# A four-layer GNN kernel on one core: fifteen spare matmuls behind each item of the two GGNN passes

## What is computed

```python
h = relu(x @ node_proj_w.T + node_proj_b)
for l in range(2):
    trans = einsum('nh,tdh->tnd', h, edge_W[l])       # 8 edge types
    msgs = trans[edge_type, src]                      # one row of 128 per edge
    agg = segment_sum(msgs, dst)                      # 200000 edges into 6250 nodes
    h = relu(gru_cell(agg, h, ...))
y = h @ out_w.T + out_b
```

## Time and profile before

| | us |
|---|---|
| device time, median of 3 runs | 12535.24 (12531.92 to 12542.11) |
| span of the profiled execution, first to last instruction | 10787.3 |
| the two GGNN passes within the span, first to last product | 2806 to 6783 |
| busy in the span: PE / DVE / POOL / ACT | 6086.2 / 5239.6 / 4871.8 / 1520.2 |

### The profile page before, as it was taken

One profiled execution on the slowest core, in us unless ns is written; L12 is line 12 of the kernel. 1 busy time (PEld: TensorE's weight loads), 2 busy tenths in 40 slices (PEclk: granted clock), 3 DMA queues, 4 the chain that ended last, 5 costly groups with the idle time before them and its releaser, 6 DMA issues. The chain is left out here.

```text
span 10787.3 us, 166167 instructions
## 1 busy us (share of the span) xinstructions
PE 6086.2 (56%) x60710; PEld 5248.2 (49%) x60711; DVE 5239.6 (49%) x7210; ACT 1520.2 (14%) x4256; POOL 4871.8 (45%) x5701
## 2 busy tenths in 40 slices
PE   4666659997433334443333333586999635545554
PEld 3333339995233333323333333486999634444444
DVE  7888878885211111121122222597888743323333
ACT  3666640001100000000000000132000001101101
POOL 2111110001577777757777777001000147777775
PEclk7777779998666666666666666555999867767776
DMA  1000032223222122221111111475322112222222
GB/s 46 0 0 0 0 46 83 83 83 118 79 66 66 53 66 66 66 72 53 52 52 52 52 52 52 163 292 190 112 93 92 63 54 79 79 80 79 73 79 73
DMA packets 322858, 798.38 MB, mean 74 GB/s; under 512 B 157570, under 2 KB 196012, under 8 KB 303436
## 3 DMA queue, kind: packets, MB, share of 16 engines
q1 hardware_dynamic: 147804, 423.30, 11.6%
q0 software_dynamic: 153216, 312.49, 10.2%
q10 hardware_dynamic: 21744, 61.34, 1.4%
HBM read 714.98 MB, written 81.79 MB: 74 GB/s over the span
## 5 line engine op out<-in xcount | busy, mean ns | idle before, releaser
L984 POOL DMA_INDIRECT ggnn_edges_G<-trans_d,ggnn_edges_rid x3136 | 2975.5, 949 | 1199.3 <-issue 955.1
L1097 PE MATMUL ggnn_edges_PS<-ggnn_edges_OH,ggnn_edges_G 128*128 128x128 f32 x6272 | 1176.8, 373 | 2317.1 <-DMA ggnn_edges_G<-trans_d,ggnn_edges_rid 2207.2
L1097 PEld LDWEIGHTS ggnn_edges_PS<-ggnn_edges_OH,ggnn_edges_G 128*128 128x128 f32 x6272 | 1136.7, 285 | 2361.7 <-issue 2360.2
L984 POOL DMA_INDIRECT mpnn_edges_G<-msg_d,mpnn_edges_rid x1568 | 1499.8, 956 | 659.5 <-issue 473.0
L1053 DVE TENSOR_TENSOR acc<-acc,ggnn_edges_PS 128x128 f32 x224 | 64.6, 288 | 2510.7 <-PE ggnn_edges_PS L1097 2510.7
L1081 PE MATMUL mpnn_edges_PS<-wt_late,mpnn_edges_at 128*128 128x256 f32 x1568 | 545.3, 522 | 682.1 <-DVE mpnn_edges_G L1040 339.9
L620 ACT ACTIVATE prep_OJF<-prep_OJ,prep_fld 128x98 bf16<-128x98 bf16 x3136 | 848.9, 362 | 555.0 <-DVE prep_OJ L676 555.0
L1081 PEld LDWEIGHTS mpnn_edges_PS<-wt_late,mpnn_edges_at 128*128 128x128 f32 x1568 | 414.8, 272 | 794.1 <-DVE mpnn_edges_G L1040 361.1
L826 PE MATMUL prep_PS<-prep_OJF,prep_OHr 128*128 128x490 bf16 x1582 | 580.7, 549 | 211.5 <-DVE prep_OHr L705 211.5
L1040 DVE TENSOR_TENSOR mpnn_edges_G<-mpnn_edges_G,mpnn_edges_PS 128x1792 f32<-128x1792 f32 x112 | 226.3, 2020 | 878.9 <-DMA mpnn_edges_G<-msg_d,mpnn_edges_rid 702.0
L1018 DVE SCALAR_TENSOR_TENSOR ggnn_edges_OH<-dstI,ggnn_edges_itm,ggnn_edges_PS 128x896 f32<-128x896 f32 x448 | 491.6, 1144 | 228.7 <-issue 164.1
(11 more groups left out here) (454 smaller groups left out, 10933.6 us busy)
## 6 DMA issues: line engine op xcount, KB each, us to landing
ba_rows<-slot_d SPq DMA_DIRECT2D x49, 3136.0 KB, 11.4
HB<-slot_d SPq DMA_DIRECT2D x49, 1568.0 KB, 6.3
heads_rows<-slot_d SPq DMA_DIRECT2D x49, 1568.0 KB, 6.3
ggnn_edges_G<-trans_d,ggnn_edges_rid POOLq DMA_INDIRECT x3136, 2.5
mpnn_edges_at<-in_edge_attr SPq DMA_DIRECT2D x112, 448.0 KB, 3.6
trans_d<-gcn_edges_tb ACTq DMA_DIRECT2D x49, 512.0 KB, 2.7
trans_d<-ggnn_edges_tb ACTq DMA_DIRECT2D x49, 512.0 KB, 3.0
mpnn_edges_G<-msg_d,mpnn_edges_rid POOLq DMA_INDIRECT x1568, 2.5
```

The costliest lines, as they stand in the source:

```text
L984: pool.indirect_dma_start(G[:, s, c, :], None, table, bass.IndirectOffsetOnAxis(ap=rid[:, s, c:c + 1].bitcast(U32), axis=0)).then_inc(gath ...
L1097: mm = pe.matmul(wp[s % 2], G[:, s, c, :], OH[:, s % 2, c, :], start=c == 0, stop=c == GC - 1)
```

## The change

In the passes without `rest` and `attr`, which are the two GGNN passes, PE issues 15 more matmuls behind the 14 products of each item: the identity as weights, 512 columns of the constant `wt_late` as the moving operand, float32, into bank 0 of PSUM. They raise no semaphore and wait for none, and nothing reads what they write; the chunk's end overwrites it. They stand behind `product` and ahead of the next item's waits, and behind a chunk's last item ahead of the wait for `acc_ready`.

```diff
@@ -877,6 +877,8 @@
                 with eng.Fori(t0, t1) as i:
                     body(i)
 
+        SPARE = 15
+
         def aggregate(name, table, index, stage, rest=None, attr=False, sl=SL):
@@ -1096,6 +1098,9 @@
                                 for c in range(GC):
                                     mm = pe.matmul(wp[s % 2], G[:, s, c, :], OH[:, s % 2, c, :], start=c == 0, stop=c == GC - 1)
                                 mm.then_inc(product, 1)
+                                if not rest and not attr:
+                                    for _ in range(SPARE):
+                                        pe.matmul(PS[:, 0, :], ident[:], wt_late[:, 0:512], start=True, stop=True)
```

## The result

The change makes the kernel slower by twice the forecast: 13157.67 us against 12538.67 of the kernel before in the same set of runs, +619 us, ratio 1.0488 (interval 1.0474 to 1.0502). The forecast was +310, and its range ended at 12960.

A forecast was written before the change was run, and what follows sets the result against it. POOL's gather issue, 17.47 us per item, was taken to bound the passes; behind each first chunk PE's serial items and chunk ends would add 151 and 159 us: 12535 + 310 = 12845 us, range 12760 to 12960.

The forecast's parts named there:

- the 1747.9 us outside as unchanged: Whole kernel: timed median 12535.24 us less profiled span 10787.3 was taken to lie outside the span and stay the same.
- Part 2: GGNN passes: PE's 16.2 us fits under POOL's 17.5 per item, but 20 us won back per chunk cannot cover some 44 lost.
- An item of 16.2 us: PE in the GGNN passes: 3.2 us of products plus 12.9 us of spares per item, ends 16.1 and 16.6.
- Clock: PE in items with spares: full clock, granted near 1.00 outside the chunk ends, against 0.61 in plain items.
- It is POOL that will be waiting: GGNN passes behind the first chunk's end: PE is never level again, so POOL waits for `added`.
- A chunk's end of 45.0 and 47.8 us: First and second GGNN pass: time from a chunk's last spare to the next product, cold start included, six per pass.
- The sum: Both GGNN passes: 96 item periods, 6 chunk ends and one more item each; +151 and +159 us, together +310.
- Its instructions cost nothing: PE's loop body in the GGNN passes: growth to 928 records is free, as in GCN's 980; otherwise 56 us.
- It stays hidden: GGNN passes: spares at one record each, or timed gathers over 9% slower, fit under POOL; no change, 12539 us; chance 6%.
- Warm clock: PE's products in the GGNN passes: if on the path, the faster clock gives back 415 us, 12120 us; chance 2%.
- A clock that stays low: PE in the GGNN passes: at 1.2 GHz an item takes 32 us, +3850 us, 16400 us in all; chance 3%.
- One that drops: PE in the GGNN passes: clock low a tenth of the time adds 1.6 us per item, 300 us in all; chance 4%.

The follow-up runs named there:

- the kernel with the pause: Kernel before, with POOL pausing (six memsets, each waited for) behind each item's 14 gathers in the GGNN and MPNN passes: 12342.95 us, ratio 0.9863, upper level.

## Why the prediction was wrong, by its own steps

- **The step that failed: "the 1747.9 us outside as unchanged".** The numbers to doubt it stood side by side: no wait, launch or load outside a span had been shown to last 1.7 ms, and the time and the span came from different runs. They were inside, as slow stretches: 1630 us between first and last gathers of three passes. With them the premise of Part 2, that an item takes POOL 17.47 us and that POOL never waits, didn't hold for the timed runs: POOL waits 1260.1 us for the row numbers.
- **POOL bounds the passes.** Right at the lower level. At the upper level POOL and PE bound each other in turn: PE is slow until POOL's slots are full, and then POOL stands still until PE has caught up.
- **An item of 16.2 us.** Right: 16.00, at both levels between slow stretches. The spare is 13.04 us for 30 records, 0.43 each, as taken from the earlier trace rows; the products took 3.13 against 3.2.
- **Clock.** Right: full clock in items with spares; 0.99 in the lower level's profile of the change in the 258 us from 3126, across a whole chunk, and 0.61 in plain items. The row, columns as in the earlier trace rows:

```profile
3126.00:3384.00 258.00, 257.64 (x927) 143.10 (x928) 41.09 (x63) 0.00 (x0) 194.95 (x207) 0.99 0.20 53
```

- **It fits for an item and not for a pass.** Right at the lower level. In the first chunk the products start every 17.5 us behind a gather (3066.57 - 3049.15 = 17.42), and from the chunk's end on every 16.00 with no idle time: 29 waits for gathers are left of 188.
- **"It is POOL that will be waiting"; "POOL's eight slots don't help".** Wrong already at the lower level, though the sum doesn't hang on it. Within the passes of the change POOL waits once, 10.9 us at 6639.86; the rest of its 391.0 us are the starts of the passes (185.4 and 191.0) and waits of 0.3. Its gathers take 1963 and 1980 us a pass, against 1961 and 1968 without the spares. PE ends a pass 134 and 150 us later, and eight slots of 17.5 us are 140: POOL runs ahead by that much, and the time shows only where POOL has to wait for the pass to end, in the 191.0 us instead of 57.9 ahead of the second pass. So "wrong if POOL still never waits" was no sign against the sum.
- **A chunk's end of 45.0 and 47.8 us.** Near. From the first GRU record to the next product are 3126.36 - 3082.67 = 43.7 us, the cold start adds 3144.41 - 3126.36 - 16.00 = 2.05. Over a pass: (2086.6 - 262.2 - 16.1 - 96 x 16.00) / 6 = 45.4, and in the second pass 49.2.
- **The sum.** At the lower level 2086.6 us against the predicted 2103 in the first pass, and 2109.2 against 2120 in the second. The items give 96 x 0.2 = 19 us less in each, the chunk ends 2 and 8 more. In time +275 against +310: PE's serial path was right and the size 35 us off, 27 of them in the passes.
- **"Its instructions cost nothing".** True at the lower level (no idle time within the items), and the second step that failed at the upper. The price put beside it, 2 us per turn and 56 in all, was nine times too small: 15 spares of 16 columns cost 503 us. The GCN pass, from which the zero was read, was the wrong row: its products end at 2540 us and POOL's 28 gathers of that stage start at 2564. What it stood for is PE's issue alone, and what was needed was PE's issue while POOL gathers.
- **The working of the upper level.** PE's idle time of "issue" in the change is 859.8 + 137.2 us, and some 70 in the GRU; busy times of spares and products are 3025.8 - 2921.0 and 974.5 - 769.5 longer than in the lower level's run of the change, with a granted clock of 0.85 in the first pass instead of 0.97: 1067 + 310 = 1377 us. The waits for gathers are 33 us shorter, which leaves some 1350. The two passes are (2772.3 - 2086.6) + (2801.6 - 2109.2) = 1378 us longer. To some 30 us, then, the change at the upper level is the predicted serial sum with the slow stretches put in. The kernel before has its own, 512 + 531 = 1043 us. The difference, 335 us, is what the forecast lacks; with the 284 us of the lower level it gives the 619.
- **Rivals.** "It stays hidden" had the right doubt in the wrong place: it asked whether the timed gathers are slower than the profiled ones, and would have made the change free. The gathers weren't slower (943 to 949 ns); PE's issue was, and that made the change dearer. Warm clock: PE's products did shrink from 5.2 to 3.3 us and nothing came back, as forecast. A clock that stays low didn't show. One that drops didn't at the lower level; at the upper the 310 us of longer busy times are about what the prediction put for it (300); there the engine has idle time ahead of its records.

The Trainium skill, "SBUF — State Buffer", section "SBUF: two separate sides", says that PE and ACT have ports of their own and never wait on anyone. As a rule on ports the traces don't speak against it: a record keeps its 0.37 us in a slow stretch, and only the time ahead of it grows. But whoever takes it as "a gather costs PE nothing" is off by 1901 us of idle time within items in the kernel before.

What is open: what delays the others' instructions while POOL issues, why in some sets of runs only, and how the records of one engine come 0.70 us apart or a multiple of it. That DVE and SyncE begin theirs together, 1.40 us apart, points to something that the engines share, but no run tells what. One rival is untested: that the recording has a part in it. Wherever the upper level shows, its profile also lacks half or more of the landing events (23933 against 88912), in the kernel with the pause too (43285 against 88910), and every time here comes with a span and a granted clock, so none is known to be of a run in which nothing was recorded.

## What to carry over

Compare the span of a profile with the times before reading anything in it: here they differ by 1.8 us where both are of one execution (13156.04 and 13154.3), and by 1748 where they weren't of one level; then a new profile comes first. Whether an extra instruction is free has to be read from rows in which the other engines do the same as in the place of the change: read issue gaps where POOL gathers, not where PE runs alone. A spare or a pause is judged by who has to catch up: here idle time put into the bound engine made the kernel faster at one level, and 14% slower at the other.

## What was not expected of the hardware

- The same kernel has two levels, 10781 to 10796 us and 12499 to 12597 us, each stable over a set of runs, 16% apart, with equal gather durations (949 and 946 ns).
- At the upper level, records of PE, DVE and SyncE begin 0.70 us apart or a multiple of it while POOL issues gathers 1.25 us apart without a break; PE's float32 matmul records, with a weight load between them, then mostly start 2.8 us apart. It took several us of rest on POOL to end: 8.88 us of waiting (for some 25 us) or a 4.6 us pause per 14 gathers did it, 2.0 us did not.
- In the profiles of that level half or more of the DMA landings are missing (23933 events against 88912 for the same kernel), so waits for a gather show as "issue".
- At full clock a float32 product of 128x128 by 512 columns is two records 0.43 us apart, 15 of them 12.9 us, whatever the operand (identity or not).
